# A two-block image kernel on one core: p5's load and d(4) a step earlier, u behind x's factors, and a new order for the last image

## What is computed

```python
x = x + L0(_gn(x), p1, p3, p4, p5, p6)     # _gn: normalisation over groups of 4 channels
x = x + L1(_gn(x), conv_w, gamma, beta)

# L0
t1 = einsum('nchw,he->ncew', x, p1)
t3 = depthwise conv of t1 with p3 (9 x 9);  t4 = grouped conv of t3 with p4 (4 -> 4 channels, 5 x 1)
t5 = einsum('ncew,ewf->ncf', t4, p5);       t6 = conv of t5 with p6 along f (3 taps, per channel)
out = einsum('ncf,nfp->ncp', t6, rows above / same / below of x) / sqrt(3 * 128)
# L1
cH, cV, cD = haar_details(x);  up = bilinear x 2
y = einsum('bchw,oc->bohw', concat[x, up(cH), up(cV), up(cD)], conv_w)
out = relu(batch_norm(y) * gamma + beta)
```

## Time and profile before

| | us |
|---|---|
| median of 3 runs | 307.37 (307.35 to 309.02) |
| the profiled execution | 308.8 |
| its span, first to last instruction | 307.0 |

### The profile page before, as it was taken

How to read it: one execution, slowest core, us unless ns; L and a number is a source line. 1 busy time by engine, 2 the same in 40 slices (tenths; PEclk the granted TensorE clock), 3 DMA queues, 4 the chain that set the end, 5 groups by cost and what they waited for, 6 DMA issues and landing times.

```text
span 307.0 us, 6666 instructions
## 1 busy us (share of the span) xinstructions
PE 251.1 (82%) x2662; PEld 192.6 (63%) x2662; DVE 237.2 (77%) x479; ACT 200.8 (65%) x268; POOL 164.5 (54%) x186
## 2 busy tenths in 40 slices
PE   6899978998775599899999999999999998850000
PEld 3333345665645397789998899888998887630000
DVE  2899996044564767778999999998999987866992
ACT  1788722277539254764878778787787777465990
POOL 4000001987605721578888898888988889540000
PEclk9999999999969599999999999999999999995555
DMA  7996041666710700000000000000000000000798
GB/s 218 410 410 227 0 125 38 177 179 173 235 63 2 275 0 0 2 0 2 1 0 2 1 0 0 3 0 2 0 0 2 2 0 3 0 0 20 316 403 355
DMA packets 11487, 28.00 MB, mean 91 GB/s; under 512 B 2528, under 2 KB 3616, under 8 KB 11456
## 3 DMA queue, kind: packets, MB, share of 16 engines
q1 hardware_dynamic: 8624, 21.37, 19.3%
q10 hardware_dynamic: 1232, 4.46, 3.9%
q0 software_dynamic: 1600, 1.74, 2.3%
HBM read 16.39 MB, written 8.39 MB: 81 GB/s over the span
## 4 chain that ended last, share of the span: by engine, by line
PE 70%; DVE 10%; issue 6%; POOL 4%; ACT 4%; DMA 3%; SPq 0%; DVEq 0%; POOLq 0%
PE low L618 10%; PE low L230 9%; PE high L594 8%; PE low L232 8%; PE low L231 8%; DVE x_sb L972 5%; PE high L729 4%; PE high L230 4%; PE high L232 4%; PE high L231 4%; PE high L632 3%; DMA x_sb<-in_x 3%; PE high L733 3%; DVE d_split L793 2%; POOL g_lo L401 2%
## 5 line engine op out<-in xcount | busy, mean ns | idle before, releaser
L264 POOL DMA_DIRECT2D d_st<-t_sb x50 | 24.7, 502 | 52.7 <-ACT t_sb L455 52.4
L401 POOL TENSOR_TENSOR g_lo<-y_sb,g_hi 128x1024 fp32r<-128x1024 f32 x15 | 36.1, 2409 | 14.4 <-ACT y_sb L550 14.4
L377 POOL TENSOR_TENSOR g_lo<-y_sb,g_hi 128x1024 fp32r<-128x1024 f32 x15 | 35.9, 2390 | 10.2 <-ACT g_hi L510 10.2
L230 PE MATMUL low<-g_hi,t_hi 128*128 128x512 f32 x96 | 37.6, 391 | 0.7 <-DVE t_lo L892 0.7
L232 PE MATMUL low<-g_hi,t_lo 128*128 128x512 f32 x96 | 37.5, 390 | 0.0
L231 PE MATMUL low<-g_lo,t_hi 128*128 128x512 f32 x96 | 37.4, 389 | 0.0
L793 DVE TENSOR_TENSOR d_split<-d_st,d_split 128x272 fp32r<-128x272 f32 x20 | 16.1, 873 | 26.0 <-ACT d_split L467 26.0
L549 ACT ACTIVATE g_hi<-x_sb,rs 128x1024 fp32r<-128x1024 f32 x16 | 21.3, 1334 | 19.6 <-POOL rs L386 19.6
L784 DVE STREAM_TRANSPOSE xa<-x_sb 128x1024 f32<-128x1024 f32 x15 | 28.1, 1951 | 6.8 <-DMA x_sb<-in_x 6.8
L594 PE MATMUL high<-xa,p_blk 128*128 128x512 f32 x64 | 29.9, 617 | 1.0 <-DVE xa L784 1.0
L618 PE MATMUL low<-t_all,taps 32*32 32x272 f32 (+1 forms) x960 | 24.4, 407 | 6.9 <-issue 6.6
(11 more groups left out here) (136 smaller groups left out, 679.3 us busy)
## 6 DMA issues: line engine op xcount, KB each, us to landing
out<-x_sb SPq DMA_DIRECT2D x6, 1024.0 KB, 4.9
x_sb<-in_x SPq DMA_DIRECT2D x11, 512.0 KB, 10.3
x_sb<-in_x ACTq DMA_DIRECT2D x8, 512.0 KB, 12.6
taps<-in_taps SPq DMA_DIRECT2D x6, 320.0 KB, 4.1
d_st<-t_sb POOLq DMA_DIRECT2D x50, 34.0 KB, 2.5
mix<-in_mix SPq DMA_DIRECT2D x6, 256.0 KB, 4.6
out<-x_sb SPq DMA_DIRECT2D x3, 512.0 KB, 3.2
d_st<-t_sb SPq DMA_DIRECT2D x30, 34.0 KB, 3.1
```

Source lines behind the costliest of these rows:

```text
L230: nc.tensor.matmul(ps, w[0], m[0], start=start, stop=False)
L264: eng.dma_start(d_st[32 * jl:32 * jl + 32, r % DR, co].rearrange("p b k -> p (b k)"), t4_sb[32 * co:32 * co + 32, r % 2, jl].rearrange("p ...
L377: pool.tensor_tensor(g1_lo[:, W:W + HW], y_sb[:, n, :], g1_hi[:, W:W + HW].bitcast(F32), ALU.subtract).then_inc(s["g1_lo"], 1)
L401: pool.tensor_tensor(g2_lo[:, :], y_sb[:, n, :], g2_hi[:, :].bitcast(F32), ALU.subtract).then_inc(s["g2_lo"], 1)
```

## The change

- SP loads p5 in step six, between `load_taps(6)` and `load_mix(6)`, instead of behind the last shuffle; w's load goes behind the wait for all eight convolutions.
- d(4) is handled in step six behind d(3) and d(5), instead of in step seven ahead of d(6). The tiles of p5, w and u lie elsewhere in the same region.
- GpSimd makes the power of x's factors right behind its shuffles, ahead of p5's low parts; VectorE makes the factors in step six, ahead of d(6)'s and d(7)'s low parts.
- ScalarE: `g1_high(0)` and the middles of u go ahead of the copy `w_hi`. VectorE: `g1_low_first` goes ahead of u.
- Last image: VectorE makes the full form instead of ScalarE (`g2_full_last`), and z's sums instead of GpSimd (`z_columns_last`). At t = 16 the first half's statistics stand where `y_neighbours(13)` stood, and `y_neighbours(13)` goes behind `norm_factors(15)`.
- TensorE: y's four high products of image 13 go between z's high and low products of that image.

```diff
-D_AT = {3: (0,), 4: (1,), 5: (2,), 6: (3, 5), 7: (4, 6)}
+D_AT = {3: (0,), 4: (1,), 5: (2,), 6: (3, 5, 4), 7: (6,)}
+Y_FIRST = N - 3
 ...
                 load_taps(r)
+                if r == R - 2:
+                    sp.dma_start(p5_raw[:, :, :], p5_in).then_inc(s["p5_raw"], 16)
                 sp.wait_ge(s["d_mm"], mixed(r - TR, 1))
                 load_mix(r)
                 shuffle(sp, r - TR, blocks[:BY_SP], d_in)
-                if r == R - 1:
-                    sp.dma_start(p5_raw[:, :, :], p5_in).then_inc(s["p5_raw"], 16)
-                    sp.dma_start(w_raw[:, :, :], w_in).then_inc(s["w_raw"], 16)
+            sp.wait_ge(s["conv"], R)
+            sp.dma_start(w_raw[:, :, :], w_in).then_inc(s["w_raw"], 16)
 ...
                 shuffle(pool, r, blocks[BY_SP:], d_in_pool)
-            pool.wait_ge(s["conv"], R)
+            pool.wait_ge(s["gst"], 1)
+            pool.tensor_tensor(rs1[:, 1, :], rs1[:, 0, :], minus_half ..., ALU.pow).then_inc(s["gst_q"], 1)
             for jc in range(JC):
 ...
-                if t >= 2:
+                if 2 <= t <= N:
                     z_columns(t - 2)
 ...
                 act.activation(rows_of(g2_hi[:, :]), pixels, ACT.Identity, **norm).then_inc(s["g2_hi"], 1)
-                act.activation(rows_of(y_sb[:, n, :]), pixels, ACT.Identity, **norm).then_inc(s["g2_f"], 1)
+                if n < N - 1:
+                    act.activation(rows_of(y_sb[:, n, :]), ...).then_inc(s["g2_f"], 1)
 ...
             g1_full(0)
+            act.wait_ge(s["d_lo"], B * (D_ORDER.index(RS - 1) + 1))
+            g1_high(0)
+            middle_of_u(0)
+            middle_of_u(1)
             act.wait_ge(s["w_f"], 1)
             act.copy(w_hi[:, :, :], w_f[:, :, :]).then_inc(s["w_hi"], 1)
-            middle_of_u(0)
-            middle_of_u(1)
-            g1_high(0)
 ...
+                if n == Y_FIRST:
+                    y_high(n)
                 pe.wait_ge(s["g2_lo"], n + 1)
 ...
+            def y_high(n):
+                pe.wait_ge(s["y_rd"], n)
+                for hh in range(2):
+                    q = slice(HALF * hh, HALF * hh + HALF)
+                    for w in (w_hi, w_lo):
+                        pe.matmul(ps_y[:, q], w[:, 0, :], g2_hi[:, q], start=(w is w_hi), stop=False)
 ...
+            def z_columns_last():
+                b = (N - 1) % 2
+                dve.wait_ge(s["z_ev"], N)
+                rows = zh[:, b, 1:J + 1, :].rearrange("p i (b j) -> p i b j", b=2)
+                dve.tensor_tensor(rows[:, :, 0, :], z3[:, b], zp[:, :, 0:J], ALU.add)
+                link(dve.tensor_tensor(rows[:, :, 1, :], z3[:, b], zp[:, :, 2:ZP], ALU.add))
+                dve.tensor_copy(zh[:, b, 0:ZP:ZP - 1, :], zh[:, b, 1:J + 1:J - 1, :]).then_inc(s["zh"], 1)
 ...
+            def g2_full_last():
+                dve.wait_ge(s["st2_r"], N)
+                dve.wait_ge(s["g1_lo"], N)
+                dve.tensor_scalar(rows_of(y_sb[:, N - 1, :]), columns_apart(x_sb[:, N - 1, :]), rs2[:, b, 3:4],
+                                  rs2[:, b, 4:5], ALU.mult, ALU.add).then_inc(s["g2_f"], 1)
 ...
+            g1_low_first()
             u_previous(0)
 ...
-            g1_low_first()
             for t in range(N + 3):
                 if 1 <= t <= N:
                     x1_add(t - 1, 0)
                 if t == N + 1:
+                    g2_full_last()
                     g2_low_last()
-                if t >= 3:
+                if t == N + 2:
+                    z_columns_last()
+                if t == N:
+                    x1_half(t - 1, 0)
+                elif t >= 3:
                     y_neighbours(t - 3)
                 if 1 <= t <= N:
                     x1_add(t - 1, 1)
-                    x1_statistics(t - 1)
+                    if t < N:
+                        x1_half(t - 1, 0)
+                    link(x1_half(t - 1, 1))
+                    x1_moments(t - 1)
 ...
                 if 1 <= t <= N:
                     norm_factors(t - 1)
+                if t == N:
+                    y_neighbours(t - 3)
```

More of the change, by code:

```diff
@@ L121, in build @@
         p5_raw = put("p5_raw", [JC, NF])
-        at_w = cursor[0]
+        at_hi = cursor[0]
+        p5_hi = put("p5_hi", [JC, NF], F32R)
+        free_behind(6)
+        p5_lo = put("p5_lo", [JC, NF], F32R)
+        free_behind(7)
+        at_u = cursor[0]
         w_raw = put("w_raw", [4, C])
         w_det = put("w_det", [4, C])
[L125 to L128, removed]
         w_f = put("w_f", [5, C])
@@ L133, in build @@
         w_hi = put("w_hi", [5, C], F32R)
+        u_sb = put("u_sb", [2, NF])
+        assert cursor[0] <= at_hi
+        cursor[0] = at_u
         w_lo = put("w_lo", [5, C], F32R)
-        assert cursor[0] <= at_w
-        cursor[0] = at_w
-        u_sb = put("u_sb", [2, NF])
         cursor[0] = region_t
@@ L314, in _ @@
                 shuffle(sp, r - TR, blocks[:BY_SP], d_in)
-                if r == R - 1:
-                    sp.dma_start(p5_raw[:, :, :], p5_in).then_inc(s["p5_raw"], 16)
-                    sp.dma_start(w_raw[:, :, :], w_in).then_inc(s["w_raw"], 16)
+            sp.wait_ge(s["conv"], R)
+            sp.dma_start(w_raw[:, :, :], w_in).then_inc(s["w_raw"], 16)
             for r in range(RS):
                 shuffled(sp, r)
-            sp.wait_ge(s["conv"], R)
             sp.wait_ge(s["d_mm"], mixed(R - 1, 1))
@@ L364, in _ @@
                 shuffle(pool, r, blocks[BY_SP:], d_in_pool)
-            pool.wait_ge(s["conv"], R)
+            pool.wait_ge(s["gst"], 1)
+            pool.tensor_tensor(rs1[:, 1, :], rs1[:, 0, :], minus_half[:, :].broadcast_to([128, N]),
+                               ALU.pow).then_inc(s["gst_q"], 1)
             for jc in range(JC):
@@ L370, in _ @@
             w_forms()
-            pool.wait_ge(s["gst"], 1)
-            pool.tensor_tensor(rs1[:, 1, :], rs1[:, 0, :], minus_half[:, :].broadcast_to([128, N]),
-                               ALU.pow).then_inc(s["gst_q"], 1)
             def g1_low(n):
@@ L549, in g2_full_and_high @@
                 act.activation(rows_of(g2_hi[:, :]), pixels, ACT.Identity, **norm).then_inc(s["g2_hi"], 1)
-                act.activation(rows_of(y_sb[:, n, :]), pixels, ACT.Identity, **norm).then_inc(s["g2_f"], 1)
+                if n < N - 1:
+                    act.activation(rows_of(y_sb[:, n, :]), pixels, ACT.Identity, **norm).then_inc(s["g2_f"], 1)
             act.wait_ge(s["rs1"], 1)
@@ L735, in z_product @@
                 mm.then_inc(s["z_mm"], 1)
+            def y_high(n):
[4 more added lines that the diff above has]
+                        pe.matmul(ps_y[:, q], w[:, 0, :], g2_hi[:, q], start=(w is w_hi), stop=False)
             def y_product(n):
-                if n >= 1:
+                if n >= 1 and n != Y_FIRST:
                     pe.wait_ge(s["y_rd"], n)
@@ L742, in y_product @@
                     q = slice(HALF * hh, HALF * hh + HALF)
+                    if n == Y_FIRST:
+                        mm = pe.matmul(ps_y[:, q], w_hi[:, 0, :], g2_lo[:, q], start=False, stop=True)
+                        continue
                     mm = split_product(ps_y[:, q], (w_hi[:, 0, :], w_lo[:, 0, :]), (g2_hi[:, q], g2_lo[:, q]),
@@ L821, in _ @@
                     d_low(q)
-            d_low(R - 1)
[L824 to L830, removed]
+                if r == GST_AT:
+                    dve.wait_ge(s["gst_q"], 1)
+                    link(dve.scalar_tensor_tensor(rs1[:, 2, :], gs1[:, :, 0], -1.0, rs1[:, 1, :], ALU.mult, ALU.mult))
+                    dve.wait_ge(s["p6_in"], 16 * 3)
+                    link(dve.tensor_scalar(p6_sb[:, :], p6_sb[:, :], float(NF) ** -0.5, None, ALU.mult))
+                    for d in range(3):
+                        last = dve.tensor_scalar(a6[:, d, :], rs1[:, 1, :], p6_sb[:, d:d + 1], None, ALU.mult)
+                    last.then_inc(s["rs1"], 1)
+            d_low(R - 1)
             def u_views(k):
@@ L865, in x1_add, with x1_half, x1_moments @@
                 dve.tensor_tensor(x_sb[:, n, sl], x_sb[:, n, sl], ps_o[:, sl], ALU.add).then_inc(s["x1"], 1)
-            def x1_statistics(n):
+            def x1_half(n, hh):
                 b = n % 2
[L870 to L873, removed]
+                dve.wait_ge(s["x1"], 2 * n + hh + 1)
+                return dve.bn_stats(st2[:, b, 6 * hh:6 * hh + 6], x_sb[:, n, HALF * hh:HALF * hh + HALF])
+            def x1_moments(n):
+                b = n % 2
                 link(dve.bn_aggr(mv2[:, b, :], st2[:, b, :]))
@@ L918, in g1_low_first @@
                                   ALU.subtract).then_inc(s["g1_lo"], 1)
+            def g2_full_last():
+                b = (N - 1) % 2
+                dve.wait_ge(s["st2_r"], N)
+                dve.wait_ge(s["g1_lo"], N)
+                dve.tensor_scalar(rows_of(y_sb[:, N - 1, :]), columns_apart(x_sb[:, N - 1, :]), rs2[:, b, 3:4],
+                                  rs2[:, b, 4:5], ALU.mult, ALU.add).then_inc(s["g2_f"], 1)
             def g2_low_last():
```

(2 more changed lines are left out.)

## The result

| | kernel before | changed kernel |
|---|---|---|
| median of 20 runs, us | 308.06 | 306.88 |
| ratio, with its 95% interval | 1 | 0.9936 (0.9911 to 0.9960) |
| span of the profiled execution, us | 307.0 | 305.5 |

By the ratio the change makes the kernel 2.0 us faster (0.6%): the interval excludes 1, but the gain is under the 1% that the prediction took as its threshold. The ratio leaves out runs over 1.5% slower than the fastest of their kernel, among them four of the changed kernel's 20; over all runs the two medians differ by 1.2 us. The forecast was 303.1 us, 1.4% faster, with a range of 301.0 to 306.0. The time lies outside it.

A forecast was written before the change was run, and what follows sets the result against it. TensorE was taken to bound the kernel, with changes only at the entry and last images. Minus 3.8, minus 0.7 and plus 0.6 gave minus 3.9 us: 304.9, or 303.5 without a cold stretch; stated 303.1, range 301.0 to 306.0.

The forecast's parts named there:

- The wait for it stands in VectorE ahead of d(6): Entry: VectorE's wait for GpSimd's power precedes d(6), not ready before 95.8; factors ready at about 94.
- minus 3.8 us: Entry to the image loop: t5(0) earlier through d(4)'s move; minus 5.1 us if the clock stays high.
- rival (b): Clock stays high at the entry and in the last images; about 301.2 us; chance 15%.
- minus 0.7 us: Entry, p5's earlier load: one code stop shrinks, minus 1.3, another grows, plus 0.6; ends plus 1.3 and minus 2.6.
- The tail: Last images: minus 0.6 us at the high clock, plus 0.6 with the clock low, which was taken.
- the halves: Last images: image 15's statistics by halves bring its moments 0.6 us forward, without reaching the chain: 0.
- y's high products: Last images: image 13's high products fill a TensorE wait, gaining 0.25 us, not 0.94, none of it on the chain.
- 303.5 to 304.9: Whole kernel: 304.9 us in the profiled execution's terms, 303.5 for an execution without conv(7)'s cold stretch.
- (c): Entry: p5 and w_raw loads lengthen code-fetch stops by 1.3 us each, clock falls earlier; 306.7, half 305; chance 27%.

The follow-up runs named there:

- E2: The changed kernel with VectorE's five factor instructions of x back behind d(7)'s low parts; 304.42 us, ratio 0.9887 to the kernel before.
- E3: The changed kernel with both the edit of E1 and the edit of E2; 302.24 us against 307.48 before, ratio 0.9809.
- E1: The changed kernel with y_neighbours(13) and both halves of image 15's statistics in their old places; 303.87 us against 307.48 before, ratio 0.9877.
- E4: E3 with x's factors in step six, ahead of d(4)'s low parts; 302.54 us, ratio 0.9822 to the kernel before.
- E5: E3 with p5's load moved back behind the last shuffle; 301.70 us against 308.41 before, ratio 0.9798.
- E8: E3 with d(4) back in step seven; 305.55 us, ratio 0.9930 to the kernel before.
- E10: E3 without the six passes of keep_clock before t5(0); 303.02 us, ratio 0.9844 to the kernel before.
- E6: E3 without y's high products of image 13 ahead of z's low ones; 303.63 us, ratio 0.9853 to the kernel before.

## Why the prediction was wrong

**The step that failed** is "The wait for it stands in VectorE ahead of d(6), which is not ready before 95.8", with the factors "ready at about 94", and through it the entry's "minus 3.8 us". The wait was free, as said; GpSimd's power ran at 83.93. The five instructions behind it I priced at about 1 us, near the 0.9 that they took in a place where GpSimd was idle. In the same section I had written that d(4)'s low parts took 4.14 us there beside p5's low parts on GpSimd, and that d(4) leaves. That the factors come in d(4)'s stead I didn't weigh. They took 4.0 us, and d(6), whose first half ScalarE had ready at about 94.5, started at 96.93.

What follows from it, in the profiled execution: keep_clock starts 1.49 us behind the mixing (I had 0.02), and all of it runs low, where I had 2.5 of its 6 passes high. t5(0) starts 5.66 us behind the mixing, where the forecast had 3.3 and E2 and E3 took 2.7. At the start of the image loop minus 3.8 us came out as minus 1.2. By the ratios E2 puts 1.5 us on the factors' place.

The traces show the slow ones one by one. Of the four tensor_scalars three took 0.93 to 1.04 us in the changed kernel, the fourth, which starts as GpSimd's last low part ends, 0.22, and all four of E1 took 0.85 to 1.06, beside GpSimd's instructions of 1.1 us; in E4, with GpSimd idle, they took 0.17 to 0.23. The scalar_tensor_tensor ahead of them took 1.00, 0.21 and 0.16 us in the three. By what means GpSimd slows them no run shows.

The entry has d(6) and d(7) at 0.66 us a part. That is from a place without p5's low parts (102.63); no row of before shows a part of d(6) or d(7) beside them. It was not tried in the change either, where GpSimd was done when d(6) began (2.68 us for four parts). In E2, E3 and E4, where it was not done, d(6) took 3.23, 2.99 and 3.02 us, with one part of 0.97 to 0.99 in each. So d(6) beside p5's low parts cost 0.3 to 0.6 us more than the 2.65 of the prediction: a small cost, but not none.

**The clock at the entry.** I assumed a fall at 100.3 and a return at 103.7. It fell at 98.6 and came back at 105.4. In E2, E3 and E4 it did not fall here at all, behind stops of 1.6 to 1.9 us; in E5 it fell behind one of 2.19, the length that the change and the kernel before have too, and in E8 behind one of 1.91. So the fall is not settled by keep_clock's place, and rival (b)'s high clock came true in some executions only.

The price of the slow factors depends on it. From the mixing to the start of the image loop:

| | factors | keep_clock behind the mixing, us | clock in keep_clock | us |
|---|---|---|---|---|
| changed kernel | slow | 1.49 | low | 15.81 |
| E1 | slow | 0.81 | high | 13.10 |
| E5 | fast | at once | low until 99.7 us | 13.0 |
| E3 | fast | at once | high | 13.02 |

The granted clock is 0.50 where the table says low and 1.00 where it says high. Lateness alone cost 0.1 us (0.6 against E4, where u(1) isn't late), the low clock alone nothing, both together 2.8. E1 has the changed kernel's instructions at the entry, so with the same slow factors one execution kept the whole forecast of the entry and the other lost two thirds of it. How often each happens the two profiles don't tell; the ratios put the mean loss at 1.5 us (E2 against the change) and 2.1 (E3 against E1).

**The traffic.** I gave p5's move minus 0.7 us. The stop at 84.95 vanished and those at 75.7 and 79.5 grew by 0.3 us each (1.06 and 2.36), in sum 1.5 us less standing; but the mixing ended only 1.2 us earlier, and E5 shows no gain from the load's place. In E1 to E8 the stops between 75 and 90 us add up to 2.6 to 4.5 us, in the kernel before to 5.0. The 1.16 us by which the mixing ended earlier look like this term come true, and are luck: it was spread, not gain, and it was 0.7 of my 3.9.

**The tail** was forecast at plus 0.6 us and measured at plus 0.7. y_product(14) waited 2.15 us (I said about 2), group_average(15) stood right behind z(14)'s low products, the halves and y's high products brought 0 in the trace, and the clock fell. One link I had missed: ScalarE's high form of image 15 waits for y_product(14), 3.18 us. It was hidden by keep_clock, which stands in TensorE's queue behind the same product and at the low clock ended at 270.2, later than the high form at 269.5. And I hadn't said that the order itself was the loss: the other edits of the tail bring 1.3 us, and y_neighbours(13)'s new place takes 2.1 (E1).

**The sum.** 3.9 was forecast from the profiled execution; 1.6 came in the trace, 2.0 by the ratio. The difference is the entry: 4.5 forecast (3.8 and 0.7), 2.3 measured, of which 1.2 lie behind the mixing and 1.2 before its end. I then took 303.1 instead of the 303.5 to 304.9 that the terms gave, for executions whose clock falls at a kinder moment. That was 0.4 to 1.8 us in the wrong direction. Some 0.7 us of the miss lie in neither: the kernel before had a median of 307.37 in three runs and 308.06 in twenty. Of the rivals, (c) gave 305 to 306.7, nearest to the measured time, but by another mechanism: not the traffic made the entry late.

**A faster kernel.** With y_neighbours(13) and the factors back (E3) the kernel takes 0.981 of the time before, with p5's load back too (E5) 0.980. Both are faster than both kernels of this case; between the two no difference can be measured. What remains of the change is d(4) in step six (3.7 us) and the last image's full form and z's sums on VectorE (1.2 us in the trace). No run has the factors in E4's place together with p5's load back.

## What to carry to other kernels

When a small instruction is moved into a place, read what GpSimd does beside it there: the same five instructions took 4.0 us in one place and 0.9 in another, and the row that showed it (the slow neighbour that the change takes away) was in hand. An instruction moved out of the way lands in front of something: ask of each one who waits for it now, and follow that wait through every queue and every buffer that is overwritten. When a late operand makes TensorE wait before filler products that should hold its clock, price it twice: with the clock high 0.8 us of waiting cost 0.1 us here, with the clock low 1.5 us cost 2.8.

## What the runs showed of the hardware

- Five VectorE instructions of at most 128 x 16 elements in SBUF took 4.0 us beside GpSimd's subtractions of 128 x 384 elements (1.1 us each; the changed kernel and E1), and 0.9 us beside an idle GpSimd in the same step (E4).
- The fp32 tensor_scalar of 128 x 1024 elements in SBUF took 0.80 us with GpSimd all but idle (the changed kernel, 267.39) and 1.17 us beside GpSimd's z sums (E3, 262.33); the two-input subtraction of that size took 1.23 us. Both times of the tensor_scalar lie within the prediction's 0.6 to 1.4 us, which were my estimate: no row of before shows one of that size.
- The granted clock fell at the entry behind the stop ahead of the last 38 mixing products in all three executions where that stop was 2.19 us (before, the changed kernel, E5), in one of five where it was 1.91 us (E8), and in none of four where it was 1.64 us, though in one of them (E10) it fell later, in a wait of 3.27 us.
- Two executions of the same instructions at the entry differ by 1.8 us at t5(0) (E3 and E6), mostly through stops in which TensorE waits for no semaphore. That they are late code is only argued.
